# Cross attention: the order of ScalarE's exponents and copies within a round

## What is computed

```python
q = (x @ Wq + bq).reshape(Bx, Tq, num_heads, d)
k = (y @ Wk + bk).reshape(Bx, Tkv, num_heads, d)
v = (y @ Wv + bv).reshape(Bx, Tkv, num_heads, d)
att = scale * jnp.einsum('bthd,bThd->bhtT', q, k)
att = att * mask - 10000000000.0 * (1.0 - mask)
att = jax.nn.softmax(att, axis=-1)
out = jnp.einsum('bhtT,bThd->bthd', att, v).reshape(Bx, Tq, Emb)
```

## Time and profile before

| what | value |
|---|---|
| median of 3 runs | 2633.68 us (2628.91 to 2634.22) |
| the profiled execution, its own time | 2629.41 us |
| its span | 2627.6 us |
| PE busy | 2334.9 us (89%) |
| DVE busy | 1868.3 us (71%) |
| ACT busy | 1183.9 us (45%) |
| POOL busy | 1118.5 us (43%) |
| exponents of the cross attention (L1174) | 256 of 913 ns, 233.4 us |
| copies of turned units (L1192) | 512 of 440 ns, 199.7 us |
| transposes of units on PE (L571) | 1536 of 288 ns, 230.4 us |

### The profile page before, as it was taken

One profiled execution on the slowest core, in us unless ns is written; L12 is line 12 of the kernel. 1 busy time (PEld: TensorE's weight loads), 2 busy tenths in 40 slices (PEclk: granted clock), 3 DMA queues, 4 the chain that ended last, 5 costly groups with the idle time before them and its releaser, 6 DMA issues. The chain is left out here.

```text
span 2627.6 us, 37776 instructions
## 1 busy us (share of the span) xinstructions
PE 2334.9 (89%) x12440; PEld 1248.8 (48%) x12440; DVE 1868.3 (71%) x5466; ACT 1183.9 (45%) x3230; POOL 1118.5 (43%) x1084
## 2 busy tenths in 40 slices
PE   6899999999999999999776998898998898987776
PEld 3455565555655556565553444443444343343222
DVE  3477776777767777776546896878788787878555
ACT  1447365574646637366441443433433343333222
POOL 2121111211112121111002776777777777777774
PEclk8899999999999999999788999999999999999999
DMA  5000101001010000101103999999999999999998
GB/s 182 8 25 8 38 2 33 13 8 38 1 45 1 15 32 1 45 1 62 54 23 143 379 394 363 402 402 416 391 418 389 418 401 404 397 401 394 407 417 354
DMA packets 161362, 520.73 MB, mean 198 GB/s; under 512 B 17168, under 2 KB 27408, under 8 KB 161168
## 3 DMA queue, kind: packets, MB, share of 16 engines
q0 software_dynamic: 129024, 469.82, 45.0%
q1 hardware_dynamic: 30560, 46.98, 5.4%
q10 hardware_dynamic: 1584, 1.52, 0.2%
HBM read 507.71 MB, written 10.55 MB: 197 GB/s over the span
## 5 line engine op out<-in xcount | busy, mean ns | idle before, releaser
L1597 POOL DMA_INDIRECT e_rows<-in_experts,e_idx x896 | 884.2, 987 | 337.9 <-issue 286.7
L1654 PE MATMUL e_ps_out<-e_rows,e_diag 128*128 128x512 f32 x1792 | 833.9, 611 | 149.5 <-ACT e_diag L1921 149.3
L1815 DVE CUSTOM_DVE_ANT_0 e_rows<-e_rows,xn_all 128x512 f32<-128x512 f32 x896 | 567.9, 688 | 230.8 <-DMA e_rows<-in_experts,e_idx 230.6
L1654 PEld LDWEIGHTS e_ps_out<-e_rows,e_diag 128*128 128x128 f32 x1792 | 339.1, 194 | 594.1 <-issue 420.0
L1921 ACT ACTIVATE e_diag<-ident_f,e_weight 128x128 f32<-128x128 f32 x896 | 286.2, 390 | 306.3 <-DVE e_weight L1826 298.1
L989 DVE SCALAR_TENSOR_TENSOR ring<-ps_s,mask 112x750 f32<-112x750 f32 x256 | 232.7, 935 | 149.2 <-PE ps_s L560 114.0
L1174 ACT ACTIVATE ring<-ring,neg_max 112x750 f32<-112x750 f32 x256 | 233.4, 913 | 164.7 <-DVE neg_max L999 164.7
L571 PE MATMUL ps_t<-ident,ring 112*125 112x112 f32 x1536 | 230.4, 288 | 46.2 <-ACT prob_t L1192 35.9
L571 PEld LDWEIGHTS ps_t<-ident,ring 112*125 112x125 f32 x1536 | 196.4, 193 | 121.5 <-ACT ring L1174 60.0
L1916 ACT ACTIVATE e_active<-e_hidden 128x4 f32<-128x4 f32 x224 | 45.9, 205 | 457.2 <-DVE e_hidden L1815 456.9
L1192 ACT COPY prob_t<-ps_t 125x336 f32<-125x336 f32 x512 | 199.7, 440 | 92.4 <-PE ps_t L571 91.9
(11 more groups left out here) (186 smaller groups left out, 2830.9 us busy)
## 6 DMA issues: line engine op xcount, KB each, us to landing
e_rows<-in_experts,e_idx POOLq DMA_INDIRECT x896, 6.2
xn_t<-in_ctx_t SPq DMA_DIRECT2D x8, 1500.0 KB, 6.5
w_in<-in_ffn_wq SPq DMA_DIRECT2D x16, 256.0 KB, 6.2
acc<-in_x SPq DMA_DIRECT2D x8, 448.0 KB, 4.8
x_dram<-x SPq DMA_DIRECT2D x8, 448.0 KB, 3.1
acc<-x_dram SPq DMA_DIRECT2D x7, 512.0 KB, 6.3
out<-acc SPq DMA_DIRECT2D x14, 256.0 KB, 5.9
x2n_dram<-ring SPq DMA_DIRECT2D x7, 448.0 KB, 3.3
```

The source lines that it names most:

```text
L1597: pool.indirect_dma_start(rows[:, v % RING, k, :], None, table[:, :], bass.IndirectOffsetOnAxis(ap=idx[:, e:e + 1], axis=0))\
L1654: mm = nc.tensor.matmul(ps_out[t % 2][:], diag[:, HU * (v % ND) + k, :], rows[:, v % RING, k, D:], start=(s == 0 and k == 0), stop=(s == S ...
L1815: last = nc.vector.tensor_tensor_reduce(down, down, xn_all[:, t, :], 1.0, 0.0, ALU.mult, ALU.add, hidden[:, b, k:k + 1])
```

## The change

On ACT, in a round, the first two exponents come as before; then the copy of the quad weighed, the copies of the turned unit u0, the third exponent, the front's copy of place 0, the fourth exponent, the front's copy of place 1, and then the copies of u0+1, u0+2 and u0+3 as before. The programs of the other engines are as they were. The loop behind the rounds, for the last four units, isn't touched.

```diff
@@ -1195,22 +1195,25 @@
             def cross(b, following):
 
                 for q in range(NQ):
+                    u = 4 * q - 4
                     if q >= 1:
-                        for u in range(4 * q - 4, 4 * q):
-                            cross_exp(b, u)
-                            if u == 4 * q - 2 and (q, 0) in FRONT_FIRST:
-                                front(following, q, 0)
+                        cross_exp(b, u)
+                        cross_exp(b, u + 1)
+                        if (q, 0) in FRONT_FIRST:
+                            front(following, q, 0)
                     if q >= 2:
                         cross_quad_out(b, q - 2)
                     for place in range(4):
                         if q >= 1 and place in (0, 2):
-                            cross_turned(b, 4 * q - 4 + place)
+                            cross_turned(b, u + place)
                         if q >= 2 and place in (0, 2) and following is None:
                             turned_ahead(2 * (q - 2) + place // 2)
+                        if q >= 1 and place < 2:
+                            cross_exp(b, u + 2 + place)
                         if (q, place) not in FRONT_FIRST:
                             front(following, q, place)
                         if q >= 1 and place in (1, 3):
-                            cross_turned(b, 4 * q - 4 + place)
+                            cross_turned(b, u + place)
```

## The result

The changed kernel takes 2645.60 us in the median of 5 runs (2642.51 to 2655.94), the kernel before 2632.45 us in 5 (2628.43 to 2634.22). The ratio is 1.0067, with a 95% interval of 1.0050 to 1.0083: slower by 17.6 us (13 to 22) as estimated from all runs; the two medians alone lie 13.2 us apart. The profiled execution took 2645.60 us against 2629.41.

A forecast was written before the change was run, and what follows sets the result against it. PE was taken to bound the attention part; +2.21 us per batch times seven (+15.5) and -0.6 in the last batch gave about +15, so 2644.4 from the profiled execution, 2648.6 on the median; forecast 2648, range 2635 to 2660.

The forecast's parts named there:

- The bound: In the cross stages of the seven batches with a front, PE sets the pace, busy 85.9 of 90 us.
- absorbed: Rival: delayed keys products and turns eat unseen slack and PE makes it up next round; no change, about 2633, chance 0.11.
- The added wait: In rounds 2 to 7, ACT stands before the quad's copy and u0 with two exponents behind it that could have run.
- unknown cost: Earliest start of the copies of u0, taken as W + 1.88, W being the weighing's start; bounds some +2 to +27 us.
- Round by round: Delays of rounds 2 to 7 in a batch with a front, together +2.21 us, times seven +15.5 us.
- The faster rival: At the turn of u0+1, PE's waits go and nothing replaces them; -15 us, 2618, chance 0.08.
- the fall behind round 7: Rival: gathered PE idle time lowers the clock, 2.6 us per fall; one per batch +18 more, 2666, chance 0.08.
- One of the signs that I had named for being wrong: Signs: a batch takes the same 160 us, ACT finds the weighing done, or PE's cross-stage clock drops below 1.00.
- the last batch at -0.6 us: In six rounds without a front ACT never waits, and the turn of u0+2 comes at 1321.22 instead of 1321.35; about -0.6 us.
- the 15 us which I summed up: Whole kernel: +15.5 us from seven batches and -0.6 us from the last batch, about +15 us.

The follow-up runs named there:

- one between: Changed kernel with only the third exponent between the copies of u0 and u0+1, and round 7's keys copy behind u0+1; ratio 0.9899 to the kernel before.
- keys in the gap: Changed kernel with PE's keys product of round 7 moved from place 3 to place 2, where PE waits; 2635.20 us against 2628.08 for the kernel before.
- Values first: Changed kernel with the copy of the values put back ahead of the third exponent in rounds 3 and 4; ratio 1.0012 to the kernel before.
- round 7 old: Changed kernel with the old order, four exponents in a row, in round 7 of the seven batches with a front; ratio 1.0022 to the kernel before.
- three first: Changed kernel with three exponents ahead of the quad's copy and the fourth behind the copies of u0; 2625.00 us against 2628.55 for the kernel before.
- one between, rotate later: "One between" with DVE rotating the fourth projection behind the first masks of round 2; 2602.89 us against 2628.08 for the kernel before.
- last batch only: Kernel before with the change applied only in the last batch, the one without a front; ratio 0.9977 to the kernel before.
- Round 7 only: Kernel before with the change applied only in round 7 of the seven batches with a front; 2645.98 us against 2628.08 for the kernel before.
- the change again: The changed kernel run once more without an edit, on another chip; 2650.36 us against 2628.08 for the kernel before.

## Why the prediction was right, and what in it was not

*The bound.* PE sets the pace of the seven batches: every shift of an ACT copy that PE was waiting for moved the round by the same amount, in both directions, unless DVE's masks then became the later wait (round 2 of "one between", round 7 of "keys in the gap"). The "absorbed" rival is out, and with it the reading that I had put on the Trainium skill (Trainium Kernel Development and Optimization, "Performance Expectations"). That section names weight-load busy time, beside MFU (the share of peak FLOPs), as a measure of how close a kernel is to roofline; that an engine with 60% by it can take up delays was my step, and it was wrong. For how near an engine is to setting the end, the waits between its instructions decided here.

*The added wait.* ACT stands before the quad's copy and before u0, 26.1 us in the first kind, which was 8.5 before. PE's waits came out a little shorter than said, 1.11, 1.57 and 0.31 us for 1.2, 1.8 and 0.5, while the rounds grew as said. The unknown cost, the start of the copies of u0, was taken as W + 1.88; the trace shows W + 1.90.

*Round by round.* Predicted +0.18, +0.48, +0.48, +0.04, +0.30, +0.73, together 2.21; measured +0.21, +0.52, +0.52, -0.01, +0.25, +0.73, together 2.22 by the table. "Values first" and "round 7 old" show for rounds 3, 4 and 7 that the cause is the one named: put back the copy of the values, or the order of round 7, and those rounds alone return. Rounds 2, 5 and 6 weren't put back one at a time; "three first" returns all six to within 0.12 us.

*The faster rival.* Its mechanism exists, though not in the changed kernel. "One between" takes more than half of PE's waits for `prob_t` away (12.3 us left of 27.5 in "one between, rotate later"), because only one exponent then stands ahead of the copies of u0+1.

*The step that failed* is the pricing of TensorE's clock, on both sides of the sum. I had the fall behind round 7 as a rival of its own, at 0.08 and 2.6 us per fall. It came on top of the forecast instead, in 6 of 7 batches, at 12.96 - 11.32 = 1.64 us each: +9.8 us. One of the signs that I had named for being wrong, PE's clock below 1.00 in the `cross` stages, thus did come.

And I put the last batch at -0.6 us, since its rounds get hardly shorter (six times my 0.13 would be 0.8; where the clock holds they read 9.95 for 10.00). It was 3.7 us shorter in the profile, with fewer rounds drawn out by a low clock, and 6 us (0 to 13) by the runs of "last batch only". By the traces the sum would be 15.5 + 9.8 - 3.7 = 21.6 us, against 17.6 (13 to 22) and 19.7 (14.5 to 24.7) measured. That the 15 us which I summed up came near the number is in part luck: terms that I had not priced went against each other, and in the profiled execution's 16.2 us two more did, the -5.5 and the -1.6 named above.

By the Trainium skill (TensorE: Matmul & The Clock Gate, "Why this matters for your kernels") waits as short as these would leave the clock alone. The traces don't agree: it fell behind a wait of 1.57 us, in 18 of 28 such rounds.

"Round 7 only" cost the same 20 us (16 to 24) as "the change again". By the rounds and falls of its profile it should cost 13. The profiled execution was 16.5 us above that of before: 13.2, another 4.4 in the last batch (76.0 us for 71.5, at a clock of 0.81 for 0.89), and 1.1 less ahead of the first weighing. So the falls vary in number and length from one execution to the next, in the last batch as well. Four runs of each kernel don't tell their costs apart, and how often the clock falls in the runs without a trace stays open.

## What to carry to other kernels

An engine with slack is still a queue: before moving an instruction up in it, ask whether its input is there by then, because everything behind it waits too. Moving a copy up pays only if what stands between it and the next copy that the bounding engine waits for fits into time in which ACT would stand anyway (here one exponent did, two did not). A wait of TensorE that has grown long can cost more than its length: two waits of 0.50 and 0.29 us became one of 1.57 here, and where the clock fell behind it the round lost another 1.64 us.

## What the runs showed of the hardware

- TensorE's granted clock fell to its lower level behind a single wait of 1.57 us, with PE busy for 5 us on either side of it: in 6, 6, 4 and 2 of 7 batches, in four traces of three kernels. The keys product behind it took 4.48 us instead of 2.79. It didn't fall in any batch behind the waits of 1.11 us in round 2, nor behind the 1.16 us of "keys in the gap". Whether it falls differs from batch to batch with identical timing around it.
- A longer wait doesn't make the fall certain. Ahead of the eighth `cross` stage PE waits 2.4 us for `x_n`, once in each of the eleven traces. The clock fell in or behind that wait in nine and not in those of the changed kernel and "values first"; the stretch between the two weighings around it is 82.6 us in these two and 83.7 to 84.3 in the others. The wait and the stretch behind it (columns as rows 2), in the kernel before and then in the changed one:

```profile
1255.56 0.60 PE L647 MATMUL ps_t<-ident,x_n 112*128 112x112 f32 x4 [2.40 <-DVE x_n L738]
...
1255.50:1261.20 5.70, 5.64 (x20) 4.68 (x21) 1.85 (x4) 0.45 (x1) 0.00 (x0) 0.70 0.00 0
```

```profile
1275.35 0.60 PE L647 MATMUL ps_t<-ident,x_n 112*128 112x112 f32 x4 [2.40 <-DVE x_n L738]
...
1275.30:1281.00 5.70, 5.65 (x29) 4.97 (x30) 2.30 (x4) 0.45 (x1) 0.00 (x0) 1.00 0.00 0
```

- One of the chips runs this program 7% slower (2809.28 us against 2628.08), and not in the attention part: "last batch only", whose first seven batches have the old order, ran on it and had the first weighing of its last batch at 1282.39 us, the kernel before on another chip at 1283.02. The expert part differs. Stretches of it in the kernel before on the usual chip and in "round 7 old" on that one, columns as rows 2:

```profile
1500.00:2600.00 1100.00, 950.65 (x2415) 430.84 (x2415) 840.96 (x3062) 391.07 (x1151) 826.62 (x848) 0.98 1.01 401
```

```profile
1500.00:2780.00 1280.00, 1009.19 (x2444) 461.29 (x2444) 853.78 (x3112) 399.40 (x1171) 862.15 (x860) 0.90 0.93 351
```

The transfers move 351 GB/s there instead of 401, and TensorE's clock is 0.90 instead of 0.98. Which of the two is the cause wasn't tried.
